# Third phase of a two-layer recurrent kernel: loops that turn at the experts' norm, scans a step later, sine products on two engines

## What is computed

```python
xn = _layernorm(x, axis=-1)
s = _L1_attn_ref(xn, ...)          # linear attention with decay: a scan over tokens
g = _silu(_L1_ffn_ref(xn, ...))    # softmax attention, then a mixture of experts
x = x + s * g

def step(st, inp):                 # the scan: 16 heads, state 16 x 16 each
    rt, wt, kt, vt = inp
    kv = jnp.einsum('bhi,bhj->bhij', kt, vt)
    y = jnp.einsum('bhi,bhij->bhj', rt, st + uh[None, :, :, None] * kv)
    return (wt[..., None] * st + kv, y)

x = x + _attention(_rmsnorm(x, w_ln1), Wq, Wkva, Wkvb, Wo)   # 16 heads, causal, rotary
residual = x
xn = _rmsnorm(x, w_ln2)            # "the experts' norm"
return residual + _moe(xn, ...)    # 8 experts, top 2, and a shared one
```

## Time and profile before

| | us |
|---|---|
| median of 3 timed runs | 2690.0 |
| lowest and highest of them | 2686.49 and 2695.47 |
| the profiled execution | 2691.32 |
| its span, first to last instruction | 2689.5 |
| the first read of the third phase on DVE (L1547) | starts at 687.3 |
| distance of two sequences (b = 1 and b = 2, same row) | about 243 |

### The profile page before, as it was taken

One profiled execution on the slowest core, in us unless ns is written; L12 is line 12 of the kernel. 1 busy time (PEld: TensorE's weight loads), 2 busy tenths in 40 slices (PEclk: granted clock), 3 DMA queues, 4 the chain that ended last, 5 costly groups with the idle time before them and its releaser, 6 DMA issues.

```text
span 2689.5 us, 36104 instructions
## 1 busy us (share of the span) xinstructions
PE 2252.5 (84%) x9632; PEld 1219.3 (45%) x9633; DVE 1748.6 (65%) x2951; ACT 924.5 (34%) x2466; POOL 886.6 (33%) x722
## 2 busy tenths in 40 slices
PE   6887499999588898789789888977988898898877
PEld 3443266666334444453444345444434443454444
DVE  5777344443258667775867686587758676865866
ACT  2333133232126224512631361245216323622541
POOL 2113300000164326324532542264154325423531
PEclk9998699999599899999889999988998899989889
DMA  4342500010212102201220221112012102211210
GB/s 144 117 139 68 162 29 27 27 30 26 87 40 76 44 16 61 79 12 36 68 63 1 60 72 36 32 57 77 3 36 75 56 0 65 67 36 32 60 52 8
DMA packets 140003, 146.21 MB, mean 54 GB/s; under 512 B 47025, under 2 KB 99889, under 8 KB 139825
## 3 DMA queue, kind: packets, MB, share of 16 engines
q1 hardware_dynamic: 132530, 131.49, 17.2%
q0 software_dynamic: 3072, 8.41, 1.0%
q10 hardware_dynamic: 4224, 4.19, 0.5%
HBM read 116.48 MB, written 27.43 MB: 54 GB/s over the span
## 4 chain that ended last, share of the span: by engine, by line
issue 26%; PE 24%; DVE 11%; POOL 10%; ACT 2%; DVEq 0%; DMA 0%; POOLq 0%; ACTq 0%
PE bank L1304 14%; DVE arena L1672 3%; DVE arena L1665 3%; POOL arena L1900 3%; POOL arena L1905 3%; DVE arena L1652 3%; PE bank L1220 2%; PE bank L1173 2%; POOL arena L1907 2%; PE bank L1127 1%; ACT arena L1475 1%; PE bank L1200 1%; PE bank L1190 1%; ACT arena L1484 1%; PE bank L1133 1%
## 5 line engine op out<-in xcount | busy, mean ns | idle before, releaser
L1918 POOL TENSOR_TENSOR arena<-arena 128x512 f32<-128x512 f32 x256 | 343.2, 1341 | 587.0 <-DVE arena L1672 574.8
L1127 PE MATMUL bank<-arena 128*128 128x512 f32 (+2 forms) x896 | 443.5, 639 | 39.3 <-ACT arena L1436 18.3
L1304 PE MATMUL bank<-arena 128*128 128x512 f32 (+2 forms) x1312 | 448.5, 497 | 6.3 <-ACT arena L1440 6.3
L1672 DVE TENSOR_TENSOR_SCAN arena<-arena 128x512 f32<-128x512 f32 x256 | 356.4, 1392 | 12.2 <-issue 10.0
L1475 ACT ACTIVATE arena<-bank,arena 128x128 f32<-128x128 f32 (+3 forms) x512 | 266.3, 530 | 247.5 <-DVE arena L1652 247.5
L1304 PEld LDWEIGHTS bank<-arena 128*128 128x128 f32 x1312 | 256.4, 210 | 193.6 <-issue 157.1
L1173 PE MATMUL bank<-arena 64*128 64x128 f32 (+3 forms) x1024 | 223.7, 516 | 129.5 <-ACT arena L1475 119.8
L1127 PEld LDWEIGHTS bank<-arena 128*128 128x128 f32 (+2 forms) x896 | 164.1, 194 | 287.1 <-issue 231.2
L1652 DVE TENSOR_REDUCE arena<-bank 128x2 f32<-128x256 f32 (+3 forms) x256 | 207.5, 811 | 79.9 <-PE bank L1176 79.9
L1484 ACT ACTIVATE arena<-bank 128x128 f32<-128x128 f32 (+3 forms) x512 | 199.6, 442 | 121.0 <-PE bank L1190 120.9
L1190 PE MATMUL bank<-arena 128*128 128x128 f32 x1280 | 208.6, 300 | 36.9 <-ACT arena L1484 29.7
(11 more groups left out here) (201 smaller groups left out, 2963.8 us busy)
## 6 DMA issues: line engine op xcount, KB each, us to landing
arena<-values SPq DMA_DIRECT2D x256, 256.0 KB, 3.4
arena<-in_L_attn_h SPq DMA_DIRECT2D x16, 512.0 KB, 3.5
arena<-in_W1T SPq DMA_DIRECT2D x8, 1024.0 KB, 6.7
arena<-in_W2T SPq DMA_DIRECT2D x8, 1024.0 KB, 10.2
sorted_rows<-arena SPq DMA_DIRECT2D x42, 128.5 KB, 8.9
arena<-sorted_rows SPq DMA_DIRECT2D x40, 128.5 KB, 2.1
gate_rows<-arena SPq DMA_DIRECT2D x39, 128.0 KB, 1.7
s_rows<-arena ACTq DMA_DIRECT2D x8, 512.0 KB, 3.0
```

Source lines behind the costliest of these rows:

```text
L1127: last = nc.tensor.matmul(dst[rows, :], w, x, start=(n == 0), stop=(n == len(pairs) - 1))
L1304: last = nc.tensor.matmul(dst[o], w, x, start=first, stop=last_one)
L1672: nc.vector.tensor_tensor_scan(state[n % STATES][:, 1:T + 1], proj["w"][:, m, :], kv[n % 2], VEC["init"][:, m * HD + j:m * HD + j + 1], AL ...
L1918: nc.gpsimd.tensor_tensor(prods[n % PRODS], state[n % STATES][:, 0:T], proj["r"][:, m, :], ALU.mult).then_inc(prod_done, 1)
```

## The change

Three edits, all in the third phase.

1. `attention(b, final)` is split into `attention(b)`, up to the norm's scaling of `xb`, and `experts(b, final)`, from the wait for it on. The loop body becomes `experts(b)`, `before_attention(b + 1)`, `attention(b + 1)`; `attention(0)` stands ahead of the loop and `experts(7)` behind it. On DVE unit 27 moves behind the read of the transposed half.
2. `parts_by_step()` has no parts in steps 0 and 1 and deals out the 48 parts over steps 2 to 31, two parts where i % 4 is 0 or 1 and where i % 8 is 6. `reduce_state` and `read_out(0)` follow the table: reduces at steps 9, 14, 19, 24, 28, 33 where they were at 7, 12, 17, 23, 28, 33, and the read at step 26 where it was 25.
3. For n in `BY_DVE = (0, 3, 5, 7)` DVE does the sine product itself, in place in `shuf`, and POOL only adds.

```diff
-    steps, at = [[]], 0
-    for i in range(1, PSTEPS):
-        n = 2 if i % 2 == 0 or i in (1, 3) else 1
+    steps, at = [[] for _ in range(LAG)], 0
+    for i in range(LAG, PSTEPS):
+        n = 2 if i % NT < 2 or i % (2 * NT) == NT + 2 else 1
...
             with pe.Fori(0, B - 1) as b:
-                attention(b, False)
+                experts(b, False)
                 before_attention(b + 1, b)
-            attention(B - 1, True)
+                attention(b + 1)
+            experts(B - 1, True)
...
                     nc.vector.stream_shuffle(shuf[n % 2][0:rows, :], src[0:rows, :], swap).then_inc(v_read, 1)
+                    if n in BY_DVE:
+                        v.wait_ge(v_read, pre.read(b, name))
+                        nc.vector.tensor_tensor(shuf[n % 2][0:rows, :], shuf[n % 2][0:rows, :], sin[0:rows, :], ALU.mult).then_inc(rope_dve, 1)
...
                 last.then_inc(xc_done, 1)
-                unit(b, EARLY + 3)
+
+            def experts(b, final):
                 v.wait_ge(made2, post.made(b, "xc0"))
                 nc.vector.tensor_scalar_mul(xbT[:, 0, :], bank[post.bank("xc0")][:, :], VEC["w_ln2"][:, 0:1]).then_inc(v_read2, 1)
+                unit(b, EARLY + 3)
...
+                    if n in BY_DVE:
+                        g.wait_ge(rope_dve, len(BY_DVE) * b + (BY_DVE.index(n) + 1))
+                    else:
+                        g.wait_ge(v_read, pre.read(b, name))
+                        nc.gpsimd.tensor_tensor(shuf[n % 2][0:rows, :], shuf[n % 2][0:rows, :], sin[0:rows, :], ALU.mult).then_inc(rope_mul, 1)
+                        by_pool = [k for k in range(1 + NH // 2) if k not in BY_DVE]
+                        g.wait_ge(rope_mul, len(by_pool) * b + (by_pool.index(n) + 1))
                     nc.gpsimd.tensor_tensor(dst[0:rows, :], dst[0:rows, :], shuf[n % 2][0:rows, :], ALU.add).then_inc(turned_q, 1)
```

More of the change, by code:

```diff
@@ L841 @@
 EARLY = 24
+BY_DVE = (0, 3, 5, 7)
 def parts_by_step():
@@ L1296, in before_attention, with result, by_tokens, attention @@
                         product(b, name, [(spread, bonus[:, i, :])])
-            def attention(b, final):
-                full = slice(None), slice(0, T)
-                def result(name, pairs, dst):
-                    begin(b, name, post, post_read)
-                    for n, (o, w, x, first, last_one) in enumerate(pairs):
-                        last = nc.tensor.matmul(dst[o], w, x, start=first, stop=last_one)
-                    last.then_inc(made2, 1)
-                def by_tokens(name, tiles, lhs, rhs, n):
-                    result(name, [((slice(None), slice((i % 2) * D, (i % 2 + 1) * D)), lhs(i, c), rhs(c), c == 0, c == n - 1)
-                                  for i in tiles for c in range(n)], bank[post.bank(name)])
+            full = slice(None), slice(0, T)
+            def result(b, name, pairs, dst):
+                begin(b, name, post, post_read)
+                for n, (o, w, x, first, last_one) in enumerate(pairs):
+                    last = nc.tensor.matmul(dst[o], w, x, start=first, stop=last_one)
+                last.then_inc(made2, 1)
+            def by_tokens(b, name, tiles, lhs, rhs, n):
+                result(b, name, [((slice(None), slice((i % 2) * D, (i % 2 + 1) * D)), lhs(i, c), rhs(c), c == 0, c == n - 1)
+                              for i in tiles for c in range(n)], bank[post.bank(name)])
+            def attention(b):
                 def wo(half, odd, groups):
@@ L1946, in attention @@
                 for n in range(EARLY + 3, UNITS):
-                    product(n)
+                    product(b, n)
                 if not final:
```

67 lines of the change are left out of this document (37 added, 30 removed).

## The result

| | us, median (lowest to highest) | runs |
|---|---|---|
| before | 2693.4 (2686.5 to 2699.8) | 20 |
| after | 2700.3 (2686.9 to 2713.4) | 20 |

The ratio is 1.0031, with an interval of 1.0016 to 1.0047: 7 us slower, between 4 and 13. The profiled execution of the kernel after took 2709.35 us, so it is one of its longer ones, 9 above its median. Its span is 18.0 us above the profiled one of the kernel before, and 4.5 of that lies ahead of the third phase, in code that the change doesn't touch: the first read of the phase starts at 691.8, where it was 687.3. Over all profiled kernels of this document it starts between 687.1 and 695.3, so a few us of any difference between two executions can come from there.

A forecast was written before the change was run, and what follows sets the result against it. Bound stage by stage: POOL in the rotation, DVE in the attention's first steps and steps 10 to 15, a chain from step 7. Terms -5.5, +0.6, -0.4, +0.6, -0.3 gave -5.0 a sequence, -40 us over 8: 2650 (2634 to 2672).

The forecast's parts named there:

- nothing there: Steps 10 to 14 and their like: eight parts before and after, so no change in time.
- 0 for three parts covered: Steps 7 to 9, 15 to 17, 23 to 25: DVE's waits of 2.70, 4.28, 2.05 us hide one moved part each step.
- 0.3 for the clock: Steps 4 to 6: PE no longer idles 5 us, so its granted clock may stay up; 0.3 us gained a sequence.
- First stretch, -5.5 a sequence: Last rotation to `highest(7)`: 1.67 turn, 0.33 wait, 3.2 for two scans and an outer, plus 0.3: -5.5 us.
- less stretching: First scan and outers behind the rotation: DVE's operations stretch less beside POOL, 0.3 us gained a sequence.
- The turn at the norm, 0: Loop turn at the experts' norm: covered by idle time of PE, ACT and DVE; cost 0, from -0.1 to 1.6 us.
- The sine products, +0.6: Rotation: four products on DVE, two meeting POOL's adds, less waits for POOL; +0.6 us a sequence, from -0.3 to +2.5.
- 4.8 for `read_out(0)`: Step 26: the read moves from ahead of DVE's wait to a stretch DVE bounds; +0.6 us a sequence.
- the reduces moved, -0.4: PE's queue around `weigh_values` of steps 18 and 10: 0.9 us gained and 0.5 lost, together -0.4 a sequence.
- The signs that the prediction named for this step: DVE's waits at steps 10, 18 and 26 should shrink to about 1.5, 2.5 and 1.5 us, not vanish.
- The one for "slower": Attention: later reduces hold POOL's product buffers, so DVE stops three times a sequence, 4 us each; 2746 us, chance 5%.
- the parts don't hide: Chain in each group of 8 steps not fixed, so 3.1 us return; gain 2 a sequence, 2674 us, chance 7%.

The follow-up runs named there:

- scan-first kernels: Parts re-dealt so pairs from step 8 run scan, outer: kernel after 2639.8 us; with all sine products on POOL 2649.5; kernel before with this table only 2649.7.
- outers first: Kernel before with a table from step 1 pairing each outer with the scan behind it, turn and sine products unmoved: 2725.5 us, ratio 1.0119.
- narrow product: Kernel after with POOL's product cut to 128 of its 512 columns, sums left incomplete: 2622.3 us, ratio 0.9727.
- six products more: Kernel after with six unread matrix products a sequence added on PE, in steps 5 to 8, 15 and 16: 2673.4 us, ratio 0.9916.
- scan-first table on the kernel before: Kernel before with only the parts table changed: parts from step 2, pairs as scan then outer; turn and sine products unmoved: 2649.7 us, ratio 0.9823.
- six extra products: Kernel after with pairs dealt as scan, outer, plus six unread PE products a sequence in steps 5 to 8, 15 and 16: 2644.0 us, ratio 0.9787.
- seventh product: Kernel after with pairs as scan, outer and six unread PE products, plus one in `before_attention` where PE waits for ACT: 2615.0 us, ratio 0.9691.

## Why the prediction was wrong

It forecast 2650 (2634 to 2672) and the kernel took 2700. Two of its terms failed, both of edit 2: "nothing there" for steps 10 to 14 and their like, which cost 20 us, and the pair of "0 for three parts covered" and "0.3 for the clock", in whose place the stretches h7 to h10 and h15 to h18 cost 28 us (16.4 + 11.9), most of it by a lower granted clock. The gain of the first stretch came as forecast. Step by step:

- **First stretch, -5.5 a sequence: right.** `highest(7)` comes 13.62 us behind the start of the last rotation; 13.5 was forecast, 19.9 it was. Over eight sequences it is -49.4 us, with 44 forecast. The scan-first kernels take the edits apart: the moved turn is worth 11.0 us there (six turns of 1.67 are 10.0), and the sine products on DVE 6.9 (111.4 to 104.5), where the prediction had 0.3 a sequence, 2.4, for less stretching. So that term was too small. The rows that were named as the sign:

```profile
1037.30 0.67 DVE L1730 TENSOR_TENSOR arena<-bank,arena 128x512 f32<-128x512 f32 x1
...
1038.53 0.94 DVE L1661 TENSOR_REDUCE arena<-bank 128x2 f32<-128x768 f32 x1
1039.39 1.67 DVE L1681 TENSOR_TENSOR_SCAN arena<-arena 128x512 f32<-128x512 f32 x1
...
1050.92 1.21 DVE L1661 TENSOR_REDUCE arena<-bank 128x2 f32<-128x1024 f32 x1
```

`highest(2)` follows the shuffle at once, with no "issue", and PE's longest wait there is 1.5 us where it was 5.02.

- **The turn at the norm, 0: right.** The answers to the earlier trace rows are these; from PE's transposes to the gate's first operation it is 6.37 us in both kernels (1146.72 to 1153.09, and 1148.34 to 1154.71), and DVE's last wait has shrunk from 3.98 to 2.28, because unit 27 lies there now.

```profile
1148.34 1.97 PE L1134 MATMUL bank<-arena 128*128 128x128 f32 x8 [4.90 <-DVE arena L1788]
...
1149.90 0.75 DVE L1793 TENSOR_SCALAR arena<-bank,arena 128x512 f32<-128x512 f32 x1 [1.61 <-PE bank L1134]
...
1154.71 0.19 DVE L1803 TENSOR_TENSOR arena<-bank,arena 128x32 f32<-128x32 f32 x1 [2.28 <-PE bank L1304]
```

- **The sine products, +0.6: right in size for the rotation** (+4.1 over eight, 0.5 each). Two of the four meet POOL (1.74 and 1.66 us at 1030.53 and 1035.12), as the queues had been walked. Alone, with what it gives in the first stretch, edit 3 was 10 us faster.

- **"Steps 10 to 14 and their like have 8 parts before and now, so nothing there": this step failed.** The count was right and the order inside it wasn't looked at. It was +8.7 us over eight sequences in h10 to h15, and +16.6 in h26 to h31, where the prediction had 0.6 x 8 = 4.8 for `read_out(0)`; that one measured 0.68 a sequence, 5.4. What is left, 8.7 + 11.2 = 20 us, is the outers behind the start of POOL's product, 25.6 us longer in the two stretches, less 6.3 that the scans got shorter. The runs with scans first, with outers first and with the narrow product show it from three sides.

The evidence stood among the rows: 1.65 at 1026.73 and the longest of 1712. The pair `outer, scan` was there too, in its harmless form, 0.70 us behind a `highest` of 0.96. The Trainium skill's rule ("SBUF — State Buffer", "Who interferes with whom": a DVE instruction with two SBUF inputs and a GpSimd instruction that reads SBUF exclude each other, and the later one waits) was set against the four products of edit 3 and not against the 48 parts that edit 2 moved. The traces agree with it and show which is later: 0.16 us decide between 0.66 and 1.67.

- **"0 for three parts covered by the waits", and 0.3 gained by the clock: this failed by the clock.** At the full clock the cover held in h15 to h18 (8.75 against 8.79) and but for 0.6 us in h7 to h10 (9.45 against 8.82). What the prediction called the granted clock's part, a gain of 0.3 in steps 4 to 6, had the wrong sign for the whole: those steps did rise from 0.74 to 1.00, but DVE bounded them, so that brought little. The lower level came in the next stretches instead, and these are a chain through PE. Against the same kernel with six products more, it costs 11.2 us in h7 to h10 and 25.0 in h15 to h18. That the reduces moved, -0.4, can't be seen beside this. The signs that the prediction named for this step spoke against it: DVE's waits at steps 10, 18 and 26 were to shrink to 1.5, 2.5 and 1.5 us, and in sequence 1 they are 0.85, 4.17 and 0. The first and the last went to the moved parts and the long outers, and the middle one kept its length because PE's chain got longer (`weigh_values` took 4.06 us instead of 2.33).

- **The rivals.** The one for "slower" named POOL's ring of products and the reduces; neither stopped DVE. POOL was the cause in another way, by being busy at the wrong moment, not by being late. The case "the parts don't hide" gave 2674 and comes nearest in its words, but its mechanism, a chain that has no slack, isn't what was seen. So the loss was in none of the cases, and 6% for slower was too little for a change that moves 48 instructions against another engine's.

Two things stay open. Why the granted clock moved when edit 2 was made, and not just that it did, the runs don't say. The extra products show that what PE is given in these steps changes it, and the narrow product that POOL's part does. But short outers alone don't keep it up: the scan-first table on the kernel before has 42 outers over 1.1 us and still takes 11.6 us at 0.71 from h15 to h18 in seven of eight sequences. And the sum of the stages is +13.6 us in the profiled executions, where the medians are 7 apart; the kernel after varies by 26 us from run to run, before by 13, which fits with a granted clock that falls in some executions and not in others, though only one execution of each has its stages on record.

## What to carry to other kernels

When a table deals work out to steps, compare not only how many instructions stand in each step but what each of them now starts beside: an operation of DVE that reads two SBUF tiles cost 0.66 us just ahead of POOL's and 1.4 to 1.7 just behind it, and one choice of order was worth 63 of 2700 us. Put such an operation straight behind the one that releases POOL, and a PSUM-reading one between the others. And when an edit takes idle time out of PE's queue at one place, read the granted clock of all the later stretches that a PE chain bounds: here the same edit raised it where DVE was the bound and lowered it where PE was.

## What the runs showed of the hardware

The same queue at the same place had two outcomes. In the kernel after, PE's 28 pieces of the projections behind equal waits, in sequences 2 and 3:

```profile
1220.29 21.36 PE L1128 MATMUL bank<-arena 64*128 64x512 f32 x28 [1.66 <-ACT arena L1441]
...
1469.38 16.36 PE L1128 MATMUL bank<-arena 64*128 64x512 f32 x28 [1.66 <-ACT arena L1441]
```

That is 5.0 us in one block, and the stretch from copy to norm is 50.9 or 45.9 us by it, at a granted clock of 0.83 or 0.93. It fell in two of seven sequences after, in four with scans first and in all seven with the six extra products; with the seventh product, in the wait ahead of this block, none of the seven took over 46. A change of some tenths of a per cent can therefore come from such blocks alone, and only the granted clock by stage tells it apart from the edit's own work.
